# Two differential attentions: gather by transposes, and another order of work inside an item

## The reference

```python
q, k, v = split(x @ w_qkv); q1, q2 = halves(q); k1, k2 = halves(k)
a1 = softmax(q1 @ k1.T * scale); a2 = softmax(q2 @ k2.T * scale)
a = a1 - lam * a2
out = a @ v                       # per head
out_n = out / rms(out) * norm_w * (1.0 - LAMBDA_INIT)
x = x + reshape(out_n) @ wo
```

## Time and profile before

| | |
|---|---|
| runs | 1841.4 to 1845.9 us, median 1843.8 us |
| profiled execution, span from first to last instruction | 1772.1 us |
| around the span (median less span; the profile has no whole time of its own execution) | 71.7 us |
| TensorE busy | 1485.7 us (84%) |
| VectorE busy | 1042.7 us (59%) |
| ScalarE busy | 941.1 us (53%) |
| reduces of the maxima, L2270, 384 | 450.0 us, 1217 ns each |
| exps, L2164, 768 | 409.7 us, 605 ns each |
| value matmuls, L2026, 1536 records | 204.6 us busy, side by side |
| gather matmuls, L2037, 256 records (8 per gather) | median 275 ns each |
| keep copies, L2276, 32 | median 442 ns each |

### The profile page before, as it was taken

One profiled execution on the slowest core, in us unless ns is written; L12 is line 12 of the kernel. 1 busy time (PEld: TensorE's weight loads), 2 busy tenths in 40 slices (PEclk: granted clock), 3 DMA queues, 4 the chain that ended last, 5 costly groups with the idle time before them and its releaser, 6 DMA issues. The chain is left out here.

```text
span 1772.1 us, 27542 instructions
## 1 busy us (share of the span) xinstructions
PE 1485.7 (84%) x9070; PEld 794.3 (45%) x9129; DVE 1042.7 (59%) x2279; ACT 941.1 (53%) x2173; POOL 386.6 (22%) x526
## 2 busy tenths in 40 slices
PE   4797667999999968684699999998598786999989
PEld 4345653555555567584222222223397452323245
DVE  6477532343433454423888888885722667888566
ACT  3454434444444444222388888887322434888743
POOL 1231540000000054474130202010277000212100
PEclk8697787999999979697699999999699897999989
DMA  2000744120300073753330303000364304223000
GB/s 79 5 1 8 226 122 123 21 72 1 72 1 1 6 227 114 228 172 105 92 84 1 84 1 103 1 1 2 123 183 119 97 9 133 70 57 75 1 1 24
DMA packets 96726, 125.97 MB, mean 71 GB/s; under 512 B 14560, under 2 KB 65376, under 8 KB 96208
## 3 DMA queue, kind: packets, MB, share of 16 engines
q1 hardware_dynamic: 86704, 105.49, 21.0%
q0 software_dynamic: 7936, 16.27, 3.4%
q10 hardware_dynamic: 1952, 2.49, 0.6%
HBM read 87.41 MB, written 36.80 MB: 70 GB/s over the span
## 5 line engine op out<-in xcount | busy, mean ns | idle before, releaser
L2270 DVE TENSOR_REDUCE MAXI<-psum 128x2 f32<-128x1024 f32 x384 | 450.0, 1217 | 69.8 <-PE psum L1995 68.3
L2164 ACT ACTIVATE EX<-psum 128x512 f32<-128x512 f32 x768 | 409.7, 605 | 97.8 <-PE psum L2016 97.0
L2760 ACT ACTIVATE EX<-psum 128x512 f32<-128x512 f32 x256 | 149.3, 599 | 172.1 <-PE psum L2690 172.1
L2698 PE MATMUL psum<-EX,N 128*128 128x512 f32 x512 | 239.0, 610 | 0.0
L2016 PE MATMUL psum<-QM,KM 64*128 64x512 bf16 x768 | 219.5, 388 | 8.7 <-DVE REST L2261 1.2
L2026 PE MATMUL psum<-EX,VST 128*32 128x512 f32 x1536 | 204.6, 604 | 4.0 <-ACT OT L2178 3.3
L1995 PE MATMUL psum<-KM,QS 64*128 64x512 bf16 x768 | 174.9, 406 | 39.1 <-DVE MAXI L2270 19.8
L2813 DVE COPY OT<-psum 128x512 f32<-128x512 f32 x64 | 44.3, 692 | 187.6 <-PE psum L2698 187.6
L2698 PEld LDWEIGHTS psum<-EX,N 128*128 128x128 f32 x512 | 93.3, 192 | 120.0 <-issue 119.6
L1147 POOL DMA_INDIRECT m_XG<-rows,m_ROWS x124 | 120.8, 974 | 105.0 <-DVE m_ROWS L1375 54.8
L1183 PE MATMUL psum<-m_XT,m_W 128*128 128x128 f32 x992 | 140.2, 287 | 0.0
(11 more groups left out here) (340 smaller groups left out, 2022.9 us busy)
## 6 DMA issues: line engine op xcount, KB each, us to landing
m_W<-in_w_dram SPq DMA_DIRECT2D x124, 256.0 KB
parts<-PART SPq DMA_DIRECT2D x24, 384.0 KB, 2.6
m_DOWN<-in_w_dram SPq DMA_DIRECT2D x32, 256.0 KB, 4.6
parts<-PART SPq DMA_DIRECT2D x24, 256.0 KB, 2.5
rows<-N SPq DMA_DIRECT2D x16, 256.0 KB, 3.0
N<-y SPq DMA_DIRECT2D x16, 256.0 KB, 4.1
QS<-parts SPq DMA_DIRECT2D x32, 128.0 KB, 3.9
QS<-parts SPq DMA_DIRECT2D x14, 256.0 KB, 5.9
```

What stands on the lines that cost most here:

```text
L2164: act.activation(EX[:, n % 2, kt, MAPS[j], :], bank_of(("score", n, i)), ACT.Exp, scale=SM_SCALE).then_inc(S["exp"].sem, 1)
L2270: dve.tensor_reduce(MAXI[:, n % 2, qt, columns], pair(i), AX, ALU.max, negate=True).then_inc(S["reduced"].sem, 1)
L2698: last = pe.matmul(banks[4 + j], N[:, n // per_b * TB + kt, :], EX[:, n % 2, kt, j, :], start=kt == 0, stop=kt == TB - 1)
L2760: act.activation(EX[:, n % 2, kt, j, :], bank_of(("score", n, i)), ACT.Exp, scale=SM_SCALE, accum_out=SUMS[:, n % 2, j, kt:kt + 1]).then_i ...
```

## The change

Gather loses the matrix `SEL` (its table, its buffer and its load) and becomes four TensorE transposes against the identity, which fill a whole bank of [tokens, 128] per tile. Keep then picks the columns in use out of that bank: in kind 2 by two copies, one for each of the group's items, in kind 3 by one copy. The tables of places change in both kinds: `AHEAD_OF`, `AT_PLACE`, `AT_VALUE`, and in kind 2 `AT_GATHER`; take moves from behind e0 to behind e1. No buffer is added or made larger.

```diff
--- before.py
+++ after.py
@@ -100,13 +100,6 @@
         c[f"fixed{k}"] = np.concatenate([everywhere(np.concatenate(cols))] + per_row + [everywhere(np.arange(n))],
                                         axis=1).astype(np.float32)
     c["f3sel"] = np.repeat(np.tile(np.eye(E, dtype=np.float32), (3, 1)), H3, axis=1)
-    for kind, dv, group in ((2, 8, 2), (3, 16, 1)):
-        sel = np.zeros((P, group, 4, dv + 1), np.float32)
-        for q in range(group):
-            for j in range(4):
-                at = 32 * j + 16 * q
-                sel[at:at + dv + 1, q, j] = np.eye(dv + 1, dtype=np.float32)
-        c[f"sel{kind}"] = sel.reshape(P, group * 4 * (dv + 1))
     return c
 
 
@@ -1774,7 +1767,6 @@
         GROUP = {2: 2, 3: 1}[kind]
         groups = items // GROUP
         per_bg = per_b // GROUP
-        GW = 4 * GROUP * W
         copies = (((0, (0, 1, 2)), (1, (3, 5)), (2, (4,))), ((0, (2, 3, 4)), (1, (1, 5)), (2, (0,))))
         stage = ExitStack()
 
@@ -1785,7 +1777,6 @@
         WV = sb("WV", [P, C])
         WO = sb("WO", [P, C])
         NW = sb("NW", [P, C] if kind == 2 else [P, 1])
-        SEL = sb("SEL", [P, GW])
         MIX = sb("MIX", [P, 4])
         half_slots = slots // 2
         buffers = 2
@@ -1810,8 +1801,7 @@
         eps = 1e-6 if kind == 2 else float(np.finfo(np.float32).eps)
         ONT = V[:].rearrange("p t c -> p (t c)")
         TUNED = REST[:, 0, :].rearrange("p (t c) -> p t c", c=C)
-        aux = [(WQK[:], f"wqk{kind}"), (WV[:], f"wv{kind}"), (WO[:], f"wo{kind}"), (NW[:], f"nw{kind}"),
-               (SEL[:], f"sel{kind}")]
+        aux = [(WQK[:], f"wqk{kind}"), (WV[:], f"wv{kind}"), (WO[:], f"wo{kind}"), (NW[:], f"nw{kind}")]
         BO = None
         if kind == 2:
             LAM = sb("LAM", [P, 4, 8])
@@ -1858,14 +1848,14 @@
             return b + 1 if g == {2: 2, 3: 0}[kind] and b + 1 < B else None
 
         LEAD = 12
-        AHEAD_OF = {2: (0, 2, 4, 6, 7, 10, 12, 13), 3: (0, 2, 3, 6, 6, 10, 12, 13)}[kind]
-        AT_PLACE = (11, 14)[:stacks]
-        AT_VALUE = {2: (4, 9, 11, 14), 3: (4, 9, 12, 14)}[kind]
+        AHEAD_OF = {2: (0, 2, 3, 6, 7, 10, 12, 14), 3: (0, 2, 4, 6, 7, 8, 12, 14)}[kind]
+        AT_PLACE = {2: (12,), 3: (11, 12)}[kind]
+        AT_VALUE = {2: (4, 8, 11, 14), 3: (4, 9, 11, 14)}[kind]
         AT_VALUE_LAST = (1, 3, 5, 6)
         AT_VALUE_OWN = (9, 11, 14)
-        AT_TAKE = 0
+        AT_TAKE = 1
         AT_TAKE_LAST = 7
-        AT_GATHER = 7
+        AT_GATHER = {2: 6, 3: 7}[kind]
         AT_KEEP = 4
         AT_PROJECT = (3, 7)
 
@@ -2034,8 +2024,7 @@
                     bank_free(("gather", u, 0))
                     out = bank_of(("gather", u, 0))
                     for qt in range(TB):
-                        last = pe.matmul(out[:, qt * GW:(qt + 1) * GW], OT[:, qt * P:(qt + 1) * P], SEL[:],
-                                         start=True, stop=True)
+                        last = pe.transpose(out[:, qt * P:(qt + 1) * P], OT[:, qt * P:(qt + 1) * P], self.ident[:])
                     last.then_inc(S["gathered"].sem, 1)
 
                 def vectors(b):
@@ -2273,9 +2262,11 @@
                 def keep(u):
                     b, g = divmod(u, per_bg)
                     dve.wait_ge(S["gathered"].sem, S["gathered"].at(u + 1))
-                    dve.tensor_copy(OS[:, b % 2, :, 4 * GROUP * g:4 * GROUP * (g + 1), :],
-                                    bank_of(("gather", u, 0))[:, 0:TB * GW].rearrange("p (t j w) -> p t j w", t=TB, w=W)
-                                    ).then_inc(S["kept"].sem, 1)
+                    turned_out = bank_of(("gather", u, 0)).rearrange("p (t j s) -> p t j s", t=TB, j=4)
+                    for q in range(GROUP):
+                        at = 4 * (GROUP * g + q)
+                        last = dve.tensor_copy(OS[:, b % 2, :, at:at + 4, :], turned_out[:, :, :, 16 * q:16 * q + W])
+                    last.then_inc(S["kept"].sem, 1)
 
                 def post(b, k):
```

## The result

The changed kernel takes 1825.2 us (1823.9 to 1831.3, 4 runs) against 1843.0 us (4 runs): ratio 0.9909, 95% interval 0.9888 to 0.9930, so 13 to 21 us less. The forecast was 1825.0 us, and -18.8 us of change; the ratio gives -16.8.

A forecast was written before the change was run, and what follows sets the result against it. No engine is full; each item is bound by a chain of waits between engines. Terms -10.2, -7.4 and -1.2 give -18.8 us: span 1772.1 becomes 1753.3, plus 71.7 around it, 1825.0 us; range 1816 to 1834.

The forecast's parts named there:

- Kind 2's items: Items walked in the new order: 10.23 us without a gather, 10.81 with, from 10.46 and 11.40.
- projection items: Three kind 2 items whose first projection moved out of a wait of TensorE: +.3 us each, +.9 in all.
- Kind 3: Items, all with a gather, walked in the new order: 11.47 us against 12.04, 13 items, -7.4 us.
- The gather: Four transposes hold TensorE .59 us, .43 less than eight passes; in the old order little of that is kept, .11.
- Rival 1: Only the gather's cut pays and the new order is neutral: -4.2 us, 1840 us; chance .08.
- rival 3: The gather's transposes run one behind the other, 1.09 us: only -6.9 us in all, 1837 us; chance .03.
- Keep: Kind 2's two copies of 144 columns on VectorE take .5 us, hidden behind other work.
- The tails: After the last items, the shorter gather stands in a row with nothing beside it: -1.2 us over both kinds.
- The sum: Whole kernel: -10.2, -7.4 and -1.2 make -18.8 us, giving 1825.0 us.
- Rival 2: VectorE nears its own pace; items fall to 10.0 and 10.5, kind 3 to 11.2: 29.3 less, 1814.5 us; chance .10.
- Rival 4: At an item's start, the new order of reduce inputs and scores starves ScalarE: slower, +8 us, 1852 us; chance .04.
- signs to look for: In the new profile: periods of 10.2, 10.8 and 11.5 us, gather .59, less ScalarE idle, no waits for `OS` or `QM`.

The follow-up runs named there:

- the late gather: Kind 2's gather moved back to its old, later place, against the changed kernel; ratio 0.9952 (0.9935 to 0.9968) to the kernel before.

## Why the prediction was right

**Kind 2's items: right, by its own steps.** Walked 10.23 and 10.81, measured 10.20 and 10.87. From s15 to V1 and from V1 to s15 (5.36 walked, 995.24 + 10.87 - 1000.75 = 5.36 measured) every step is where the walk had it. Removing parts gave back what the walk said for the take (11.10, walked 11.15), V1 in plain items (10.48, walked 10.5) and the late gather (11.03, walked 11.05). Three removals came out otherwise than walked, each by a wait that the walk had missed or mis-timed: the place (the wrong sign), V1 in items with a gather (11.44, walked 11.15), and P2 in projection items (12.80, walked 12.4). The term was -10.2. From the first V3 to the 30th the profiles give -11.3 (11 x .53 + 3 x .94 + 11 x .26, less 3 x .08 for projections), and item 2 .3 more (10.56 to 10.23), together -11.6. Two sizes were off: projection items cost .08 and not .3, and three items that carry `post` fell from 11.81 to 10.87, which I had counted like the others.

**Kind 3: right in kind, too large.** Walked 11.47, measured 11.56. The 13 periods give -6.3 (.48 in most, .39 in the two with a projection, .36 in the last, .64 in two others), and item 2, which I had left out, takes .27 longer (11.13 to 11.40): the term is -6.0 instead of -7.4. Of the .09, .07 are the take: V0 came .76 behind it, and I had walked .67, as for an exp. The items with a gather in kind 2 are .06 longer than walked by the same. That kind 3's own moves (P4, P5, P6, V2 and the places) each pay was not tested: no run took one of them back alone, nor P7's in kind 2.

**The gather: right.** .58 for .59, and nearly nothing alone (.13 an item in kind 2, walked .11; 0 or .07 in kind 3). Rival 1 is refuted by the periods, rival 3 by 999.41 to 999.99: four transposes cost .58 us while the record of one takes .27. The Trainium skill, "TensorE: Matmul & The Clock Gate", "PE-mode transpose", gives its 275 ns in a sentence on bf16 transposes, which the prediction did not say; these are fp32, and the figure agrees with their record (273 ns), not with what they cost.

**Keep: right.** Behind V1, with at least .43 us to spare.

**The tails: wrong.** Forecast -1.2. Kind 2's end, forecast at -.35, gained nothing: from the last exp to the matmul on `m_UPCOUNT` in the block that follows it took 25.30 us before and 25.35 after (first profile of each). The gather is shorter there, and TensorE waits .83 us instead of .55 for VectorE soon after it. In kind 3 the step "take, gather, keep stand in a row with nothing beside them" failed: VectorE is busy with the residual of two batches there, and the gather was never what it waited for. The row that says so is the DVE timeline of the end, which I had not read. With the clock's fall the term was +2.6 or more in ten of the eleven profiles of kernels with an edit.

**The sum.** -11.6, -6.0 and +2.6 make -15.0, within the interval of -13 to -21, and 2 us from the ratio's -16.8. That the -18.8 came within 2 us of it too is in part luck: kind 2 was put 1.4 too small, kind 3 1.4 too large, and the tails 3.8 too good. Rival 2 did not come: items stopped at 10.2, not at 10.0. Rival 4: P2 ahead of s3 costs plain items nothing, and helps projection items.

**Of the signs to look for,** V3 to V3 came close to what was said (10.20, 10.87 and 11.56 for 10.2, 10.8 and 11.5), the gather to the next matmul too (.58), P2 goes 1.92 after s15 and not over 2.2, the granted clock is .99, and no score waited for `OS`.

No variant beat the changed kernel. P2 back ahead of s4 is level with it.

## What to carry to other kernels

Where three engines hand work round in a loop, walk one period by distances of starts, and put the wait for a free bank into the walk of every matmul, by its place in the ring: one that was left out turned a walked gain of .1 into a loss of .3 to .4 an item. A shorter operation pays only when the order leaves its end on the path, and a new order pays more with operations short enough to fit its waits (here 10.6 us without and 14.9 with the short gather), so try the two together. And read every engine's row of a tail before counting on one of them.

## What the runs showed of the hardware

- Two executions of one program on one core differed by some 70 us while both attentions were alike to about 1 us; in 220 us of the routed blocks the DMA engines moved 168 and 149 GB/s. The quick one came once in fourteen profiles, and its cause is open.
- Four transposes of 128x128 fp32 hold TensorE .58 us, where four fp32 matmuls with 72 columns and the same stationary operand hold it 1.02.
- Kind 3's first item took 12.2, 13.1 or 14.8 us in executions with the same order, with 0, 3 or 9 us of clock at 1.2 GHz from its first exp on. Such steps at the edges of a stage are as large as the effects sought here, so single whole times told less than the periods.
- In a stretch of nine microseconds the granted clock was .62 or .99 with the same instructions; six more matmuls in an idle time 3 us ahead of it changed nothing.
- Two VectorE copies of 144 columns out of PSUM, 9 columns out of every 32, cost .05 us more than one of 288 in a row.
